# Six units of a CIN tower's first rounds in another mix of fp32 and split products, and another PSUM bank and half distance in its last rounds

## The reference

```
z   = einsum('bfd,bgd->bfgd', x, h)
cur = relu(einsum('bfgd,fgl->bld', z, Wr) + b)      # 39 x 39 or 39 x 64 pairs, 128 outputs
h, direct = cur[:, :64], cur[:, 64:]                # the last layer keeps all of it as direct
y   = relu(relu([sum of directs over d, dense] @ W_top1 + b_top1) @ W_top2 + b_top2) @ W_top3
```

## Time and profile before

| | us |
|---|---|
| median of 3 runs | 1288.57 (1287.99 to 1289.71) |
| the profiled execution, its time | 1284.82 |
| the profiled execution, its span | 1282.8 |
| PE busy | 1213.8 (95%) |
| DVE busy | 1113.0 (87%) |
| POOL busy | 1037.6 (81%) |
| ACT busy | 816.2 (64%) |

### The profile page before, as it was taken

One profiled execution on the slowest core, in us unless ns is written; L12 is line 12 of the kernel. 1 busy time (PEld: TensorE's weight loads), 2 busy tenths in 40 slices (PEclk: granted clock), 3 DMA queues, 4 the chain that ended last, 5 costly groups with the idle time before them and its releaser, 6 DMA issues.

```text
span 1282.8 us, 14379 instructions
## 1 busy us (share of the span) xinstructions
PE 1213.8 (95%) x4180; PEld 768.0 (60%) x4180; DVE 1113.0 (87%) x1274; ACT 816.2 (64%) x1115; POOL 1037.6 (81%) x629
## 2 busy tenths in 40 slices
PE   0588999999999999999999999999999999999979
PEld 0344666666666666666666666666666666676645
DVE  2199999999999999999999999999999989999843
ACT  1146666666667666766666666766666778877643
POOL 7578888888888888888888888888888778888813
PEclk9999999999999999999999999999999999999989
DMA  9194455665444556655455556665545556553000
GB/s 185 31 245 102 96 129 143 147 146 138 114 116 117 120 132 147 146 147 131 107 120 119 122 139 146 147 146 120 117 117 118 120 141 145 144 144 109 16 1 1
DMA packets 102510, 156.17 MB, mean 122 GB/s; under 512 B 20811, under 2 KB 32988, under 8 KB 102322
## 3 DMA queue, kind: packets, MB, share of 16 engines
q1 hardware_dynamic: 92256, 152.56, 49.5%
q0 software_dynamic: 10176, 2.70, 2.1%
HBM read 151.31 MB, written 6.19 MB: 123 GB/s over the span
## 4 chain that ended last, share of the span: by engine, by line
PE 81%; DVE 7%; issue 4%; POOL 4%; ACT 4%; DMA 0%; DVEq 0%; ACTq 0%
PE curM L980 37%; PE curM L1005 13%; PE curM L997 13%; PE curM L998 13%; DVE z L611 4%; POOL emb L341 3%; ACT h L843 2%; PE xk L969 2%; DVE zl L689 1%; DVE zl L698 1%; ACT zh L809 1%; DVE curY L677 1%; PE h L1097 0%; PE h L1105 0%; PE curY L980 0%
## 5 line engine op out<-in xcount | busy, mean ns | idle before, releaser
L352 POOL TENSOR_TENSOR zl<-z,zh 128x1024 fp32r<-128x1024 f32 (+1 forms) x301 | 718.4, 2397 | 149.9 <-ACT zh L809 138.5
L611 DVE TENSOR_TENSOR z<-xr,h 128x1024 f32<-128x1024 f32 x456 | 548.5, 1212 | 3.6 <-ACT h L843 2.9
L980 PE MATMUL curM<-z,wf 128*128 128x512 f32 (+3 forms) x1228 | 540.7, 600 | 0.9 <-ACT h L843 0.8
L809 ACT ACTIVATE zh<-z 128x1024 fp32r<-128x1024 f32 (+1 forms) x320 | 337.8, 1057 | 290.0 <-DVE z L611 236.5
L997 PE MATMUL curM<-zh,wl 128*128 128x512 f32 (+1 forms) x828 | 380.7, 460 | 5.4 <-ACT zh L809 3.2
L341 POOL DMA_INDIRECT emb<-in_tbl_dram,idx x312 | 312.6, 1002 | 84.2 <-issue 52.1
L980 PEld LDWEIGHTS curM<-z,wf 128*128 128x128 f32 (+3 forms) x1228 | 216.1, 188 | 238.9 <-issue 216.3
L998 PE MATMUL curM<-zh,wh 128*128 128x512 f32 (+1 forms) x828 | 326.5, 394 | 0.0
L1005 PE MATMUL curM<-zl,wh 128*128 128x512 f32 (+1 forms) x828 | 260.4, 396 | 14.4 <-DVE zl L689 6.9
L843 ACT ACTIVATE h<-curM,bias 64x512 f32<-64x512 f32 x372 | 240.4, 646 | 20.0 <-DVE z L611 10.0
L689 DVE TENSOR_TENSOR zl<-curY,zh 128x512 fp32r<-128x512 f32 x240 | 164.8, 687 | 66.7 <-ACT zh L794 65.9
(11 more groups left out here) (125 smaller groups left out, 359.7 us busy)
## 6 DMA issues: line engine op xcount, KB each, us to landing
xr<-xT SPq DMA_DIRECT2D x384, 192.0 KB, 6.1
xs<-xT SPq DMA_DIRECT2D x279, 156.0 KB
xq<-xT SPq DMA_DIRECT2D x64, 256.0 KB, 7.1
emb<-in_tbl_dram,idx POOLq DMA_INDIRECT x312, 4.5
xs<-xT SPq DMA_DIRECT2D x62, 78.0 KB
xT<-xc SPq DMA_DIRECT2D x31, 78.0 KB
xr<-in_L_rec_W_dram SPq DMA_DIRECT2D x16, 144.0 KB, 6.8
xT<-xc SPq DMA_DIRECT2D x31, 40.0 KB
```

What stands on the lines that cost most here:

```text
L352: nc.gpsimd.tensor_tensor(zl[0:n, SNUM[r, u] % NL, :], z[0:n, z_slot(r, u), :], zh[0:n, SNUM[r, u] % NH, :], ALU.subtract).then_inc(lo_poo ...
L611: return nc.vector.tensor_tensor(z[:, slot, :].rearrange("p (a n) -> p a n", a=2), x, h, ALU.mult)
L809: nc.scalar.activation(zh[0:n, SNUM[r, u] % NH, :], z[0:n, z_slot(r, u), :], ACT.Copy).then_inc(hi_ready, 1)
L980: mm = nc.tensor.matmul(cur[:, :], wf[rows, full_at(u), a, :], z[rows, z_slot(r, u), a * N:(a + 1) * N], start=start and i == 0, stop=stop ...
```

## The change

The four P units become a new kind E in rounds -1 and 0 (six units in all: 1 and 6 of round -1; 1, 6, 12 and 17 of round 0). An E unit has no low part: PE adds, per tile, the high weights by all of z (fp32) and the low weights by the high part (fp32r). Round 31 keeps D.

HALF is replaced by `half_lag(r)`: 1 in round 30, 2 in the others. In round 30 DVE and ACT go on with a P unit's second half one unit later instead of two, and DVE subtracts the second half two units later instead of four.

Layer 2 of round 29 is contracted into xk instead of curM[0]. PE's waits follow: round 30 begins without the wait for read2, unit 10 of round 29 waits until xk has been read, and the top layers wait for read2 of step 29.

```diff
-HALF = 2
@@
     if k == "P":
-        return "P" if r in IN_PSUM else "D"
+
+        return "P" if r in IN_PSUM else "E" if r < 1 else "D"
@@
-def behind(r, u, n):
-
-    ru = ORDER[NUM[r, u] - n] if NUM[r, u] >= n else None
-    return ru if ru in HALVES else None
+def half_lag(r):
+
+    return 1 if r == STEPS - 2 else 2
+
+
+def behind(r, u, halves):
+
+    for n in (1, 2):
+        at = NUM[r, u] - n * halves
+        if at >= 0 and ORDER[at] in HALVES and half_lag(ORDER[at][0]) == n:
+            return ORDER[at]
+    return None
@@
-            return curM[(r + (layer - 1) % 3) % 2]
+
+            return xk[:, :] if (r, layer) == (STEPS - 3, 2) else curM[(r + (layer - 1) % 3) % 2]
@@
-                if before is not None and kind(*before) == "F":
+                if before is not None and kind(*before) in "EF":
                     dve.wait_ge(z_used, NUM[before] + 1)
@@
-                    second, finished = behind(r, u, HALF), behind(r, u, 2 * HALF)
+                    second, finished = behind(r, u, 1), behind(r, u, 2)
@@
-                second = behind(r, u, HALF)
+                second = behind(r, u, 1)
@@
+                    if kind(r, u) == "E":
+                        pe.wait_ge(z_ready, NUM[r, u] + 1)
+                        for a in range(n):
+                            nc.tensor.matmul(cur[:, :], w_high[:, w, a, :].bitcast(F32), z[:, z_slot(r, u), a * N:(a + 1) * N],
+                                             start=start and a == 0, stop=False)
                     pe.wait_ge(hi_ready, SNUM[r, u] + 1)
+                    for a in range(n if kind(r, u) == "E" else 0):
+                        mm = nc.tensor.matmul(cur[:, :], w_low[:, w, a, :], zh[:, h, a * N:(a + 1) * N], start=False,
+                                              stop=stop and a == n - 1)
+                    if kind(r, u) == "E":
+                        mm.then_inc(z_used, 1)
+                        return
@@
-                        if u == 0 and r >= 1:
+                        if u == 0 and 1 <= r <= STEPS - 3:
                             pe.wait_ge(read2, r)
+                        if u == 0 and r == STEPS - 2:
+                            pe.wait_ge(read0, 7 * STEPS)
@@
-                        if u == A_END and 1 <= r <= STEPS - 3:
+                        if u == A_END and 1 <= r < STEPS - 3:
                             pe.wait_ge(read0, 7 * (r + 3))
+                        if u == A_END and r == STEPS - 3:
+                            pe.wait_ge(z_ready, NUM[r - 1, UNITS - 1] + 1)
+                            pe.wait_ge(xc_copied, STEPS)
@@
             pe.wait_ge(top_loaded, 16 * 6)
+            pe.wait_ge(read2, STEPS - 2)
             pe.wait_ge(read0, 7 * STEPS)
```

More of the change, by code:

```diff
@@ L460, in round_ @@
                         for u in range(A_END + 3 * k + 1, A_END + 3 * k + 4):
-                            if kind(r, u) == "P" and u + HALF > A_END + 3 * k + 3:
+                            if kind(r, u) == "P" and u + half_lag(r) > A_END + 3 * k + 3:
                                 sp.wait_ge(z_second, HALVES[r, u] + 1)
```

## The result

| | before | after |
|---|---|---|
| median | 1288.28 us (1287.27 to 1309.78) | 1292.65 us (1291.15 to 1306.24) |
| ratio, with its 95% interval | 1 | 1.0055 (1.0037 to 1.0074) |
| the profiled execution: time, span | 1284.82, 1282.8 | 1292.47, 1290.4 |

A forecast was written before the change was run, and what follows sets the result against it. PE alone was taken to bound the middle, with waits and low clock at both ends. Early -3.8 and late -3.1 summed to -6.9 us: 1277.9 for the profiled execution, 1281.7 us as median, range 1279.0 to 1286.5.

The forecast's parts named there:

- Round -1: Two E units free 2.26 us of DVE, 2.2 kept; PE starts round 0 at 103.2 instead of 105.38.
- The price of an E unit: On PE, 2.18 us against 1.37 for a split unit: +0.8 us each, +4.8 for six.
- POOL's relief: Fewer DVE subtractions beside gathers bring POOL to unit 11 of round 0 about 4.1 us earlier, at 122.8.
- rival C: POOL gets nothing back in the early rounds: early +0.8, late gain -2.3, 1286.3 us; chance 0.09.
- Round 0 up to unit 13: 23.3 us of work plus 3.2 of waits and low clock, 26.5; PE ends unit 13 at 129.7, 4.6 earlier.
- the sentence on the cover: Round 0: product 13 waits for PE's unit 6, done near 118, needed near 127.5; DVE runs ahead.
- The low clock: Start of round 0: half-clock loss of 1.7 us kept, 22% of 7.70 us.
- rival F: PE keeps full clock at the start of round 0: 1.7 us more gained, 1280.0 us; chance 0.10.
- Rival B: Low clock moves into the top layers, losing 1.9 us of the late gain: 1283.6 us; chance 0.18.
- Part 2: Layer 2's bank in round 29: PE starts round 30 1.1 us earlier; worth 0, at most 1.1.
- Part 3: Half distance 1 in round 30: product 19 +5.2 us, top layers at 1228.9 instead of 1232.05, -3.1 us.
- rival D: Extra fp32 work of six E units uncovered on PE: +4.8 us early, 1290.3 to 1292.2; chance 0.09.

The follow-up runs named there:

- before_again: The kernel before, unchanged, profiled a second time: 1288.79 us, span 1286.7.
- plain_e: The changed kernel with POOL's 36 gathers of the second block replaced by plain SP transfers (embeddings partly not the reference's): 1284.62 us, ratio 0.9966 to the kernel before.
- plain_d: The changed kernel without E units, POOL's 36 second-block gathers replaced by plain SP transfers: 1284.54 us, ratio 0.9969 to the kernel before.
- e_12_17: The changed kernel with E only in units 12 and 17 of round 0: 1286.26 us, ratio 0.9980 to the kernel before.
- wait_only: The changed kernel with the six E units' arithmetic back to D, their z slots still freed by PE: 1286.45 us, ratio 0.9982 to the kernel before.
- e_round_m1: The changed kernel with E in units 1 and 6 of round -1 alone: executions 1286.08 to 1305.74 us, ratio 1.0042 to the kernel before.
- late_only: The changed kernel with all six E units back to D, keeping the bank and half-distance changes: 1286.77 us, ratio 0.9979 to the kernel before.
- early_only: The changed kernel with the bank and half-distance changes taken back, leaving the six E units: 1297.72 us, ratio 1.0060 to the kernel before.
- gathers_first: The changed kernel with POOL's 36 second-block gathers issued right behind the first block's: 1328.10 us, ratio 1.0306 to the kernel before.

## Why the prediction was wrong, step by step

**Round -1: right.** 2.2 us were forecast, 1.97 came (28.29 to 26.32), and PE's E units fitted into the waits for subtractions.

**The price of an E unit: right.** From 140.18 to 142.34 are 2.16 us (2.18 forecast), and units 14 to 23 grew by 0.83 for unit 17.

**POOL's relief: right, but it bought nothing.** POOL's gathers ended at 125.94 instead of 130.87, 4.9 us earlier (4.1 forecast), and the gathers that are stretched are those beside DVE's subtractions (1.79 us at 120.40, beside the subtraction at 120.16), not those beside products. So rival C's premise is refuted, as is the inference of the Trainium skill (SBUF — State Buffer, "Who interferes with whom") behind it. Of the 4.9 us some 1 us (one stretched gather) is no relief by the change: the subtraction of unit 7 fell behind the gathers because DVE stood. Stretched is a gather that begins while a subtraction already runs; the one at 100.30, which began 0.13 us before a subtraction, kept its 0.94. But then POOL waited 5.52 us for ACT, and its first subtraction began at 131.47, not at or before 122.8.

**Round 0 up to unit 13: the failed step.** Forecast were 26.5 us, measured 36.20. With the prediction's own split of this stretch:

| | before | forecast | after |
|---|---|---|---|
| work | 20.9 | 23.3 | 23.3 |
| waits that the timeline shows | 5.1 | 1.4 | 7.5 |
| half clock | 1.7 | 1.7 | 5.0 |
| short gaps, the remainder | 1.2 | 0.1 | 0.4 |

(Half clock: the low part of unit 0, E unit 1 and the start of unit 2 took 2.8 us more than at full clock, the low part of unit 7 and three F units 2.2; in `before_again` it was 1.7. The 1.4 of the forecast is the wait in unit 0, for which the timeline shows 0.99 in the kernel before and 0.92 after.) The step that failed is the sentence on the cover: product 13 "waits for PE's unit (0,6), done near 118, and is needed near 127.5; DVE runs ahead there". It took a count to be there when PE is done. In fact DVE stood much earlier, at products 8 and 10. The wait of product 8 is new: before, DVE's own subtraction freed the slot of unit 1. That of product 10 for F unit 3 stands in the kernel before too, and I had never listed it, since it ended last nowhere. DVE makes that product at 120.43 in `before_again` without a stop; in after it is ready for it at 121.38, hardly later, and gets the count at 127.88.

What the gathers do to it is shown by removing them: `plain_e` needs 26.93 us for this stretch, 0.4 more than the forecast 26.5, and 69.03 against 72.14 for both rounds: -3.1 us, where the forecast had -3.8 (0.2 in round -1, 0.4 here). That this is near the sum is partly luck: PE's waits for POOL, 3.2 us of the stretch, are gone in `plain_e` because the gathers are, whatever the E units do. `plain_d` is as good without E (68.62). Without gathers the E units save 1.97 us in round -1 and cost 1.56 up to unit 13 and 0.82 behind it. So what was to be gained in round 0 was a gain against POOL's lateness, which comes from its gathers, and the same gathers took it away.

Why the count for unit 3 is 9.6 us late with E in units 1 and 6, and about 2 at most without, is only argued; the late count of unit 0 in `e_12_17` and `wait_only` says that E units make lateness longer or make it cost, not that they alone cause it. Of the gathers that begin between 112 and 125 us, five of seven are stretched to 1.7 to 2 us by subtractions in `before_again`, and two of ten in after, where POOL issues one every 1.25 us while DVE stands. If it is that dense issuing that holds the counts back, a first short stand (the new wait of product 8) prolongs itself until the gathers are over. No run separates this.

**The low clock: mis-sized as part of the same.** I had kept 1.7 us and, in rival F, thought of PE not losing it; 5.0 us came, 2.2 of them behind the standstill of 6.16 us, the rest at the start of round 0. Rival B's remark that waits as long as those for POOL aren't followed by half clock doesn't hold in general: in `e_round_m1` the wait of 1.83 us in unit 11 is followed by split matmuls at 0.43 us from start to start instead of 0.23 (131.25 to 134.2).

**Part 2, worth 0 to 1.1: not separated.** In `late_only` PE begins round 30 1.0 us earlier than in `before_again`, counted from the start of round -1, and then waits 1.25 us for POOL, so that the low part of unit 0 begins at the same time (1116.70 and 1116.72 us from there), as the text says; the bank alone wasn't run.

**Part 3: right, nearly to the tenth.** DVE's three gaps are 1.07, 1.07 and 1.08 us (1.16 forecast), product 19 came 5.18 us later (5.2), the copies ended 5.83 us behind its end (5.8), PE waited 0.93 us (1.2), and 3.05 us were gained (3.1), 2.6 by the medians of `late_only`. Rival B's half clock in the top layers isn't in the profile of after (granted clock 1.00 from 1225 to 1245), while in that of `late_only` it is 0.83 from 1235 to 1245.

**The rivals.** The one on the slower side, rival D, had its time nearly right (1290.3 to 1292.2) for a wrong reason: its premise was that the early waits don't end with DVE's subtractions, but without two of these round -1 became 1.97 us shorter. No rival had a wait in the place of the removed one, though the change gives DVE such waits by its own diff; 0.06 for slower was far too little for that.

## What to carry to other kernels

Before you call an engine "ahead", list what each of its next instructions waits for, the waits that the change leaves alone too, and say how far off each is if its count comes some microseconds late; beside dense gathers the distance from a producer's end to the waiter's start is to be read from the trace, not taken as nil. And if a gain is won against another engine's lateness, ask first what makes that engine late.

## What the runs showed of the hardware

- While POOL issues indirect gathers one behind the other, counts of PE reach the other engines late: 2.7, 4.2 and 9.6 us in after, 14.1 us in `early_only`, 27.6 us in `gathers_first`, and 4.0 us in `e_12_17`, where it costs nothing. I saw no such delay of DVE's or ACT's counts in the same stretches: in after PE began the low part of unit 7 (131.42) 0.05 us behind the end of DVE's subtraction. Without the gathers, PE's counts in round 0 came in time (0.04 us at product 8). Why is open, and so is whether the issue or the transfers of the gathers do it.
- The last late count came 1.9 to 3.4 us behind the last gather in five kernels, but 10.6 us lay between them in `gathers_first`; others came while gathers ran.
- A gather lasts 0.94 us, and 1.7 to 2.0 when it begins up to 0.3 us after a DVE subtraction with two operands in SBUF (in one case of `early_only`, at 92.30, it did not); one that begins before the subtraction isn't stretched, nor is one beside products, which have an operand in PSUM.
